# Product keys layer: 20 instead of 64 candidate sums per head, and 4 of 32 rows of the last head's pair sums on VectorE

## The reference, cut to what matters

```python
sim = jnp.einsum('pbnhd,hkpd->pbnhk', q, keys_p)
scores, idx = jax.lax.top_k(sim, K)
all_scores = (scores[0][..., :, None] + scores[1][..., None, :]).reshape(b, s, NH, K * K)
...
sc, pk = jax.lax.top_k(all_scores, K)
...
wd = down[indices]
hmid = jnp.einsum('bnd,bnhkd->bnhk', inputs, wd)
hmid = jax.nn.sigmoid(sc) * jax.nn.gelu(hmid, approximate=False)
wu = up[indices]
return jnp.einsum('bnhk,bnhkd->bnd', hmid, wu)
```

## Time and profile before

| what | us |
|---|---|
| median of 3 runs | 1511.5 |
| lowest and highest | 1510.49, 1514.61 |
| the profiled execution, its own time | 1514.63 |
| its span in the trace | 1512.9 |
| what lies around the span | 1.7 |
| pair sums on POOL (line 1562), 128 instructions, busy | 246.7 |
| selections on DVE (line 1484), 128 instructions, busy | 156.9 |
| candidate sums on DVE (line 1455), 16 instructions, busy | 16.5 |

### The profile page before, as it was taken

How to read it: one execution, slowest core, us unless ns; L and a number is a source line. 1 busy time by engine, 2 the same in 40 slices (tenths; PEclk the granted TensorE clock), 3 DMA queues, 4 the chain that set the end, 5 groups by cost and what they waited for, 6 DMA issues and landing times. The chain is left out here.

```text
span 1512.9 us, 23626 instructions
## 1 busy us (share of the span) xinstructions
PE 1329.7 (88%) x7572; PEld 1008.0 (67%) x7572; DVE 1072.2 (71%) x2211; ACT 921.6 (61%) x1391; POOL 878.7 (58%) x619
## 2 busy tenths in 40 slices
PE   8789999798788888779849999998898559999998
PEld 8767777456466566646638887886366448787786
DVE  5534454497599999969766666776577668777765
ACT  4467787653688887557536665555656436555554
POOL 4168888400599999922116776664155237665665
PEclk9689999899799999899779999999999679999999
DMA  7021111000000000040034346443100134444442
GB/s 254 1 58 42 49 42 35 2 2 1 1 1 0 2 0 0 0 169 2 2 75 128 127 127 176 128 128 108 77 1 1 57 88 128 124 133 122 131 123 86
DMA packets 51565, 103.34 MB, mean 68 GB/s; under 512 B 6248, under 2 KB 10928, under 8 KB 49936
## 3 DMA queue, kind: packets, MB, share of 16 engines
q1 hardware_dynamic: 51472, 102.17, 22.6%
HBM read 99.99 MB, written 2.16 MB: 68 GB/s over the span
## 5 line engine op out<-in xcount | busy, mean ns | idle before, releaser
L1562 POOL TENSOR_TENSOR RA<-RW 128x1024 f32<-128x1024 f32 x128 | 246.7, 1965 | 90.0 <-ACT RW L1523 87.8
L890 ACT ACTIVATE PS<-PS 128x512 f32<-128x512 f32 (+1 forms) x260 | 151.2, 582 | 211.5 <-PE PS L677 210.6
L995 POOL TENSOR_TENSOR l3f_hid_rest<-RW,l3f_hid_high 128x512 fp32r<-128x512 f32 x132 | 170.3, 1291 | 132.8 <-ACT l3f_hid_high L882 132.7
L995 POOL TENSOR_TENSOR l2f_hid_rest<-RW,l2f_hid_high 128x512 fp32r<-128x512 f32 x128 | 165.3, 1292 | 137.0 <-ACT l2f_hid_high L882 137.0
L995 POOL TENSOR_TENSOR l0f_hid_rest<-RW,l0f_hid_high 128x512 fp32r<-128x512 f32 x128 | 165.3, 1292 | 64.2 <-ACT l0f_hid_high L882 57.0
L948 DVE TENSOR_TENSOR RW<-RW,PS 128x512 f32<-128x512 f32 (+1 forms) x260 | 178.6, 687 | 10.6 <-DVE RW L943 0.9
L1593 PE MATMUL PS<-identf,RA 128*128 128x128 f32 x1024 | 140.7, 290 | 36.2 <-DVE RA L1484 32.0
L1593 PEld LDWEIGHTS PS<-identf,RA 128*128 128x128 f32 x1024 | 120.0, 148 | 70.9 <-DVE RA L1484 67.0
L1484 DVE SCALAR_TENSOR_TENSOR RA<-RA,RW,PS 128x1024 f32<-128x1024 f32 x128 | 156.9, 1277 | 12.0 <-ACT PS L1529 11.5
L948 DVE TENSOR_TENSOR RW<-RD,PS 128x512 f32<-128x512 f32 x128 | 87.9, 687 | 107.1 <-ACT PS L890 98.8
L1529 ACT ACTIVATE PS<-RA 128x1024 f32<-128x1024 f32 x128 | 130.1, 1026 | 54.3 <-DVE RA L1484 51.8
(11 more groups left out here) (352 smaller groups left out, 3306.2 us busy)
## 6 DMA issues: line engine op xcount, KB each, us to landing
RD<-l2f_kept SPq DMA_DIRECT2D x128, 256.0 KB, 3.6
RB<-l3f_kept SPq DMA_DIRECT2D x128, 256.0 KB, 3.8
RD<-l0f_kept SPq DMA_DIRECT2D x32, 256.0 KB, 3.1
RA<-in_w SPq DMA_DIRECT2D x2, 2048.0 KB, 10.7
RA<-in_wg SPq DMA_DIRECT2D x2, 1024.0 KB, 9.3
RA<-in_wu SPq DMA_DIRECT2D x2, 1024.0 KB, 11.3
RA<-in_wd SPq DMA_DIRECT2D x2, 1024.0 KB, 13.2
RC<-in_wg SPq DMA_DIRECT2D x1, 2048.0 KB, 8.8
```

The costliest lines, as they stand in the source:

```text
L890: act.activation(gate, gate, e.func, bias=st.bias).then_inc(e.acted, 1)
L995: pool.tensor_tensor(rest, hid, high, ALU.subtract).then_inc(e.hidden_ready, 1)
L1562: pool.tensor_tensor(*pair_scores(r, h), ALU.add).then_inc(added, 1)
```

## The change

VectorE forms 20 candidate sums per head, in four additions of 64, 56, 24 and 16 columns (8 x 8, 8 x 7, 8 x 3, 8 x 2) in place of one of 512, and searches over 20 columns in place of 64. It gets one more addition in each tile: rows 0 to 3 of the 32 rows (128 of 1024 columns) of the pair sums of head 7, between `weigh` and the first selection. GpSimd's instruction for head 7 covers the other 28 rows (896 columns). ScalarE's sigmoid of head 7 waits for both. The tally of VectorE has 4 in place of 1 for the additions.

```diff
--- before.py
+++ after.py
@@ -1411,7 +1411,9 @@
     Ssb = [k.RW[:, bass.ts(r, 512)] for r in range(2)]
     M = [k.RW[:, bass.ts(1 + r, 1024)] for r in range(2)]
     xb = [k.RW[:, bass.ts(24 + r, P)] for r in range(2)]
-    cand = k.RW[:, 3328:3840]
+    cand = k.RW[:, 3328:3328 + 20 * NH].rearrange("p (h j) -> p h j", h=NH)
+    shared_added = s("shared_added")
+    ROWS_OWN = 4
     t8 = k.RW[:, 3840:3968].rearrange("p (n j) -> p n j", j=8)
     v8 = k.RW[:, 3968:4032].rearrange("p (n j) -> p n j", j=8)
     bn = k.stats[:].rearrange("p t s -> p (t s)")
@@ -1452,11 +1454,17 @@
                     own.mark(dve.max(t8[:, j, :], Ssb[r][:, bass.ts(j, NK)]))
                 own.wait()
 
-                own.settle(dve.tensor_tensor(cand.rearrange("p (h a b) -> p h a b", h=NH, a=8),
-                                             over(t8[:, 0:NH, :], 3, 8), over(t8[:, NH:, :], 2, 8), ALU.add))
+                a, b = t8[:, 0:NH, :], t8[:, NH:, :]
+                own.mark(dve.tensor_tensor(cand[:, :, 0:8], a[:, :, 0:1].broadcast_to([P, NH, 8]), b, ALU.add))
+                own.mark(dve.tensor_tensor(cand[:, :, 8:15], a[:, :, 1:8], b[:, :, 0:1].broadcast_to([P, NH, 7]),
+                                           ALU.add))
+                own.mark(dve.tensor_tensor(cand[:, :, 15:18], a[:, :, 1:2].broadcast_to([P, NH, 3]), b[:, :, 1:4],
+                                           ALU.add))
+                own.settle(dve.tensor_tensor(cand[:, :, 18:20], a[:, :, 2:4], b[:, :, 1:2].broadcast_to([P, NH, 2]),
+                                             ALU.add))
                 dve.sem_inc(paced, 1)
                 for h in range(NH):
-                    own.mark(dve.max(v8[:, h, :], cand[:, bass.ts(h, 64)]))
+                    own.mark(dve.max(v8[:, h, :], cand[:, h, :]))
                 own.wait()
 
             def weigh(n, r, q):
@@ -1479,12 +1487,16 @@
                     add_out(n - 2)
                 if known(n, 1):
                     weigh(n - 1, 1 - r, q if t else q - 1)
+                pairs, s0, s1 = pair_scores(r, NH - 1)
+                own_rows = slice(0, ROWS_OWN)
+                dve.tensor_tensor(pairs[:, own_rows], s0[:, own_rows], s1[:, own_rows],
+                                  ALU.add).then_inc(shared_added, 1)
                 for h in range(NH):
                     dve.wait_ge(sig_ready, n * NH + h + 1)
                     dve.scalar_tensor_tensor(A[h], A[h], v8[:, h, 7:8], SG[h % 2], ALU.is_ge,
                                              ALU.mult).then_inc(g_ready, 1)
 
-            per = 2 * NH + 1 + NH
+            per = 2 * NH + 4 + NH
             for n in range(TPB):
                 step(n, n, 0)
             with dve.Fori(1, NB) as i:
@@ -1524,6 +1536,8 @@
 
             def sigmoid(n, h):
                 act.wait_ge(added, n * NH + h + 1)
+                if h == NH - 1:
+                    act.wait_ge(shared_added, n + 1)
                 if known(n, 1) or h >= 2:
                     act.wait_ge(g_ready, n * NH + h - 1)
                 act.activation(SG[h % 2], A[h], ACT.Sigmoid).then_inc(sig_ready, 1)
@@ -1559,7 +1573,8 @@
                 for h in range(NH):
                     if known(n, 1):
                         pool.wait_ge(g_turned, (n - 1) * NH + h + 1)
-                    pool.tensor_tensor(*pair_scores(r, h), ALU.add).then_inc(added, 1)
+                    first = ROWS_OWN if h == NH - 1 else 0
+                    pool.tensor_tensor(*(a[:, first:] for a in pair_scores(r, h)), ALU.add).then_inc(added, 1)
             run_tiles(pool, step)
 
         @block.tensor
```

## The result

The changed kernel takes 1585.75 us in the median of 3 runs (1581.84 to 1585.99) against 1511.5. The medians are 74 us apart, a quotient of 1.049; the ratio that the runs are given is 1.046, 95% interval 1.0431 to 1.049, which is 70 us. The change makes the kernel slower. The forecast was 1579, range 1548 to 1605. The profiled execution took 1585.75 us with a span of 1584.0, 71.1 us more than the span of before.

What follows compares the result with a forecast made beforehand. GpSimd and VectorE were both taken as full, excluding each other for whole instructions. Tiles 1 to 15 add 62.4 us and tile 0 to 1 adds 4.8, together +67: profiled 1582, median 1579, range 1548 to 1605.

Steps and rivals of the forecast that it cites:

- Who goes next: VectorE and GpSimd both queued for SBUF: first to ask is served; GpSimd gets in between two back-to-back VectorE additions.
- tile 0: First tile of the layer: the additions are hidden, as VectorE's 9.70 us wait for ScalarE holds four waits of 1.9.
- The first addition: First of VectorE's four per tile: asked for at t = 11.51, waits 0.20 us for head 3's sum, done 0.08 later.
- Rival C: First addition misses head 3's end and waits for head 4: 1.7 us more a tile, 1604 us; chance 0.06.
- The three waits: Second to fourth additions each wait for one GpSimd sum (heads 4, 5, 6), 1.77 us each; fourth done at t = 17.24.
- The rest of the picks: VectorE after the additions: wait 0.15 us, searches 0.83, output 0.32, `weigh` 1.14, four rows 0.2; next selection at t = 19.9.
- Cover elsewhere: GpSimd's slack (15 us of work in 19.9) also covers ScalarE and TensorE; TensorE idles longer, its clock dips at tile starts.
- A: VectorE's four additions keep the ports until the last is done: gain 5 us, 1506 us; chance 0.11.
- B: Some of the four additions get through in pairs, one or two waits fewer: 1552 or 1526 us; chance 0.09.

Runs made afterwards that it cites:

- e3: Kernel before the change with its one addition of 512 columns cut into four of 128, patterns and searches unchanged: 1590.49 us, ratio 1.0493.
- e5: Changed kernel without VectorE's four rows, each head's pair sums on GpSimd in two instructions of 512 columns: 1553.42 us, ratio 1.0272 to the kernel before.
- e8: Changed kernel without VectorE's four rows, second list's eight best in the second sigmoid's PSUM buffer: 1505.94 us, again 1508.03; ratios 0.9934, 0.9956 to the kernel before.

## Why the prediction was right

**Who goes next**, the step on which all hung, held: the one pair of instructions at 1235.34 and 1235.66 was enough to foresee 48 waits, 3 in each of 16 tiles. (By the kernel's lines 2053 and 2054 the two are a maximum and a minimum, and line 2063 is a comparison; the prediction calls them additions. They too have two SBUF inputs.) One pair was thin ground for a rule; that it held in every tile is what the change showed, and e3 to e5 showed it again. In tile 0 they are hidden, as forecast: VectorE waits 3.83 us for ScalarE there where it waited 9.70.

**The first addition** is asked for at t = 536.46 - 524.95 = 11.51, as forecast, and GpSimd's first sum begins at t = 529.21 - 524.95 = 4.26, forecast 4.19: GpSimd caught up and then waited for `store_s`. The addition was done at t = 11.86, forecast 11.79. Rival C, which needed it 0.20 us later, stayed away in every tile.

**The three waits** were mis-sized, the largest term that was. I took 1.77 us each, as for a sum that was itself held up, and put the fourth addition's end at t = 17.24. It is 17.41: the sums begin 1.87 us apart as if nothing had come between them. From the first addition's end to the fourth's are 5.55 us, forecast 5.45; with GpSimd's 0.07 later start that is 0.17 of the 0.2 us by which a tile is longer than forecast (20.10 for 19.9), and 15 times 0.2 is the 3 us by which 67 fell short of 70. The median was missed by 7 us, not 3: the forecast took off 3 us because the profiled execution of before was that much above its median, while the profiled execution of the changed kernel is its median. About 1 us more lies outside the tiles.

**The rest of the picks**: wait 0.16 (0.15), searches 0.86 (0.83), output 0.33 (0.32), `weigh` 1.14 (1.14), rows 0.20 (0.2). The rows' addition met an idle GpSimd in all tiles but the first: the shortened sum (1.70 us, 0.22 less than the others, forecast 0.23) ends at t = 529.21 + 14.77 - 524.95 = 19.03, forecast 18.8, and the rows are asked for at t = 19.90.

**Cover elsewhere** held. TensorE's clock did fall at the start of a tile, in the windows of one tile (us, busy time of PE, PEld, DVE, ACT, POOL, granted clock, DMA share, GB/s):

```profile
524.70:530.70 6.00, 5.10 (x22) 4.43 (x22) 5.85 (x7) 4.22 (x5) 1.49 (x1) 0.50 0.01 3
530.70:534.70 4.00, 4.00 (x31) 3.47 (x30) 4.00 (x4) 3.40 (x5) 4.00 (x3) 0.97 0.01 2
...
536.30:543.30 7.00, 3.09 (x21) 2.15 (x19) 6.78 (x14) 3.38 (x4) 7.00 (x5) 1.00 0.00 0
```

TensorE is busy 3.09 of 7.00 us while VectorE waits, and has 0.50 of its clock, 1.2 GHz, for a tile's first 6 us. It costs nothing that shows: of the tile's path only `weigh` waits for the transposes on VectorE, and the idle time ahead of it is 0.9 us in 15 tiles together. One of GpSimd's 15 waits is put down to a transpose, but its first sum begins at the same place in that tile as in the others.

**The rivals.** A, that the four additions keep the ports, is out: 1.91 to 1.94 us each. So is B, some in pairs. A gain of A's kind was real all the same, and e8 got it by moving one input out of SBUF. That 1506 was forecast for A and 1505.94 measured for e8 is luck: A has the four rows in it, and it counts from 1511.5, while the kernel before had 1516.1 beside e8. In differences, A promised 5 us, and e8 gained 10 and, once more, 6.

**Left open:** whether the engine that asked first is served or the two strictly alternate. In every row here both rules give the same.

## What to carry to other kernels

Where GpSimd is kept busy by instructions that read SBUF, count VectorE's instructions with two SBUF inputs, not their columns: each may cost the length of one GpSimd instruction, so fewer columns in more instructions can be a loss. Moving one input to PSUM takes an addition out of this, if a buffer is free at that moment and the order of the queue need not change for it. And a timeline that puts the two engines' rows side by side shows it before anything is built; the idle columns don't, since the wait counts as busy.

## What the runs showed of the hardware

A short VectorE addition between two GpSimd sums costs GpSimd nothing. Beside 512 columns a sum lasts 2.36 us instead of 1.91; beside additions of 16 to 64 columns it lasts 1.91 and the next begins on time, and beside those of 128 columns in e3 1.95 to 1.97. So with short additions the harm is one-sided, and GpSimd's row in the profile doesn't show that the two collide. An addition with one input in PSUM is no slower: 64 columns take 0.22 us in e8, beside a working GpSimd, and 0.22 in the last layer of the kernel before where two SBUF inputs met an idle one (line 2059 at 1238.34).
